# x2 turned by a DMA transpose instead of TensorE, gelu-1 remainders on VectorE, and other instruction orders, in an attention and FFN kernel

## The reference

```python
x = x + _layernorm(_L0_attn_ref(_layernorm(x), w_lhs, w_rhs))
x = x + _layernorm(_L0_ffn_ref(_layernorm(x), w1_w, w1_s, ..., w3_s))

# attention: softmax over t, no scaling
scores = jnp.einsum('nsd,ntd->nst', x * w_lhs, x * w_rhs)
return jnp.einsum('nst,ntd->nsd', jax.nn.softmax(scores, axis=2), x)

# FFN: weights are ternary (-1, 0, 1), s are scales of the outputs; hidden width 512
h = jax.nn.silu(_tlin(x, w1_w, w1_s)) * _tlin(x, w2_w, w2_s)
h = jax.nn.gelu(_tlin(h, h1_w, h1_s), approximate=False)
h = jax.nn.gelu(_tlin(h, h2_w, h2_s), approximate=False)
return _tlin(h, w3_w, w3_s)
```

## Time and profile before

| | before |
|---|---|
| time, median of 3 runs | 520.17 us (519.22 to 520.48) |
| time of the profiled execution | 520.69 us |
| its span, first to last instruction | 518.9 us |
| busy: PE / PE weight load / DVE / ACT / POOL | 469.5 / 350.3 / 366.9 / 405.8 / 314.0 us |
| share of the span | 90% / 68% / 71% / 78% / 61% |
| chain that ended last | PE 83%, ACT 6%, DVE 5%, POOL 2%, DMA 1% |
| mean granted TensorE clock | 0.975 |
| DMA | 11.83 MB, mean 23 GB/s |

### The profile page before, as it was taken

The page is one execution under the profiler, slowest core; times in us unless marked ns, Lnnn a source line. Parts: engine busy times, 40 slices in busy tenths (PEclk is TensorE's granted clock), DMA queues, the critical chain, the costliest instruction groups (busy, mean ns, idle before and its releaser), DMA issues.

```text
span 518.9 us, 8118 instructions
## 1 busy us (share of the span) xinstructions
PE 469.5 (90%) x2626; PEld 350.3 (68%) x2626; DVE 366.9 (71%) x1144; ACT 405.8 (78%) x715; POOL 314.0 (61%) x332
## 2 busy tenths in 40 slices
PE   0557599999999999999999999999999999989892
PEld 0355368686868777786868686777778686858571
DVE  3558695977777796969787777869695868654422
ACT  3343398979899898979898998989797989886871
POOL 4313409376684939395866849393958666575464
PEclk9977799999999999999999999999999999999997
DMA  8000000001010000101010100001000000000001
GB/s 302 2 1 23 21 1 1 21 1 40 3 42 0 22 21 0 42 1 42 1 42 2 40 1 22 20 2 42 1 21 0 22 3 20 1 20 2 21 1 40
DMA packets 5659, 11.83 MB, mean 23 GB/s; under 512 B 752, under 2 KB 752, under 8 KB 5616
## 3 DMA queue, kind: packets, MB, share of 16 engines
q1 hardware_dynamic: 5616, 11.28, 6.4%
HBM read 7.09 MB, written 4.19 MB: 22 GB/s over the span
## 4 chain that ended last, share of the span: by engine, by line
PE 83%; ACT 6%; DVE 5%; POOL 2%; issue 2%; DMA 1%; POOLq 0%; SPq 0%; ACTq 0%; DVEq 0%
PE hid_bank L290 46%; PE score_bank L222 8%; PE hid_bank L222 8%; PE score_bank L227 4%; PE score_bank L290 4%; PE score_bank L244 3%; PE score_bank L257 3%; PE score_bank L259 3%; PE score_bank L258 3%; DVE hA L1031 2%; ACT L803 1%; DVE row_max L992 1%; DMA columns<-columns_dram 1%; DVE max_diag L996 1%; ACT gate L764 1%
## 5 line engine op out<-in xcount | busy, mean ns | idle before, releaser
L290 PE MATMUL hid_bank<-hA_hi,w_hi 128*128 128x512 f32 x256 | 108.7, 425 | 1.4 <-DVE hA L1031 1.4
L1367 POOL TENSOR_TENSOR hB_lo<-hB,hB_hi 128x512 fp32r<-128x512 f32 x64 | 81.0, 1289 | 45.5 <-ACT hB_hi L775 45.4
L290 PE MATMUL hid_bank<-hB_hi,w_hi 128*128 128x512 f32 x256 | 101.5, 396 | 0.0
L290 PE MATMUL hid_bank<-hB_lo,w_hi 128*128 128x512 f32 x256 | 101.5, 396 | 0.0
L290 PE MATMUL hid_bank<-hA_lo,w_hi 128*128 128x512 f32 x256 | 101.2, 395 | 0.0
L1372 POOL TENSOR_TENSOR hC_lo<-hC,hC_hi 128x512 fp32r<-128x512 f32 x64 | 80.7, 1284 | 7.1 <-ACT hC_hi L775 7.1
L774 ACT ACTIVATE hC<-hid_bank,columns 128x512 f32<-128x512 f32 x64 | 44.5, 696 | 31.4 <-PE hid_bank L290 31.4
L1333 POOL TENSOR_SCALAR ln_y_var_eps<-ln_y_mean_var 128x4 f32<-128x4 f32 x16 | 3.5, 217 | 102.2 <-DVE ln_y_mean_var L959 102.2
L1031 DVE SCALAR_TENSOR_TENSOR hA<-hid_bank,columns,gate 128x512 f32<-128x512 f32 x64 | 47.6, 747 | 22.2 <-ACT gate L764 22.2
L803 ACT ACT_TABLE_LOAD x47 | 60.3, 1283 | 1.5 <-PEq L1532 0.7
L290 PEld LDWEIGHTS hid_bank<-hA_hi,w_hi 128*128 128x128 f32 x256 | 48.3, 189 | 13.1 <-DVE hA L1031 3.2
(11 more groups left out here) (85 smaller groups left out, 1150.1 us busy)
## 6 DMA issues: line engine op xcount, KB each, us to landing
x_in<-x_dram SPq DMA_DIRECT2D x16, 256.0 KB, 2.6
out_dram<-y_out SPq DMA_DIRECT2D x16, 256.0 KB, 2.0
w_raw<-weights_dram SPq DMA_DIRECT2D x5, 512.0 KB, 6.0
w_raw<-weights_dram SPq DMA_DIRECT2D x1, 256.0 KB, 5.1
columns<-columns_dram SPq DMA_DIRECT2D x1, 9.5 KB, 4.5
```

Of the source, the lines that this page charges most:

```text
L290: mm = nc.tensor.matmul(bank[:, :], lhs, rhs, start=(k == order[0] and n == 0), stop=(k == order[-1] and n == len(pairs) - 1))
L1367: nc.gpsimd.tensor_tensor(hB_lo[:, m, :], hB[:, m, :], hB_hi[:, m, :].bitcast(f32), ALU.subtract).then_inc(hB_lo_ready[m], 1)
```

## The change

Five edits.

1. **x2's transpose.** PE no longer turns x2. ACT writes the high half of `x2n` straight from SBUF into `x2_split[:, 0]` (`high_x2`, fp16), DVE the low half into `x2_split[:, 1]` (`low_x2`), and one DMA transpose from the SP queue turns both halves (128 x 1024 fp16, 256 KB) into `x2T[b % 2]`. `gated` waits for its landing.
2. **Low halves of the first gelu** (`low_B`) move from POOL to DVE, four per batch, in all batches. `low_C` stays on POOL.
3. **Orders.** The order of blocks within a sum (`SCORE_ORDER`, `BLOCKS`, `ORDER1`, `ORDER2`, `ORDER3`) may now differ by batch, and all five lists are rearranged. Batches 0 to 2 and 13 to 15 have lists of their own. The attention of a batch is spread over four places in the step instead of three.
4. **Start.** The SP queue loads weight part 2 and then x(0) first. POOL takes the first root before the weight remainders.
5. **Small ones.** `normalize_y` writes into `y_out`, and `add_ffn` adds in place. A helper `keep_warm` (matmuls that only occupy TensorE) is defined, with a POOL memset for its operand, and nothing calls it: TensorE waits in its gaps as before.

```diff
+        x2_split = sb("x2_split", [P, 2, S], f16)
+        x2T = sb("x2T", [P, TWO, 2, T, P], f16)
-        y_n = sb("y_n", [P, T, D], f32)
...
         @block.sync
+            def turn_x2(b):
+                sp.wait_ge(x2_lo_ready, b + 1)
+                after(sp, gated_mm[GATED_ORDER[b - 2][-1]], b - 1)
+                sp.dma_start_transpose(x2T[:, b % TWO, :, :, :].rearrange("p h t s -> p (h t) s"),
+                                       x2_split[:, :, :].rearrange("p h s -> p (h s)")).then_inc(
+                                           x2T_landed[b % TWO], 16)
-            def start():
-                load_weights(1)
-                load_weights(0)
-                load_columns()
-                load_weights(5)
-                load_weights(4)
-                load_x(0)
+            load_weights(2)
+            load_x(0)
+            load_weights(5)
+            load_weights(0)
+            load_columns()
+            load_x(1)
...
         @block.tensor
-            def turn_x2(b):
-                pe.wait_ge(x2n_ready, b + 1)
-                turn(x2T_bank, x2n[:, :, :], x2T_turned)
...
-                if m == GATED_ORDER[0]:
-                    pe.wait_ge(x2T_lo_ready, b + 1)
+                if m == GATED_ORDER[b][0]:
+                    pe.wait_ge(x2T_landed[b % TWO], 16 * (b // TWO) + 16)
+                hi, lo = (x2T[:, b % TWO, half, :, :].rearrange("p t s -> p (t s)") for half in range(2))
...
         @block.scalar
-            def high_x2T(b):
-                act.wait_ge(x2T_turned, b + 1)
-                after(act, gated_mm[3], b)
-                nc.scalar.copy(x2T_hi[:, :], x2T_bank[:, :]).then_inc(x2T_hi_ready, 1)
+            def high_x2(b):
+                act.wait_ge(x2n_ready, b + 1)
+                after(act, x2T_landed[(b - 1) % TWO], 16 * ((b + 1) // TWO))
+                nc.scalar.copy(x2_split[:, 0, :], flat(x2n)).then_inc(x2_hi_ready, 1)
...
         @block.vector
-            def low_x2T(b):
-                dve.wait_ge(x2T_hi_ready, b + 1)
-                minus(x2T_lo[:, :], x2T_bank[:, :], x2T_hi[:, :]).then_inc(x2T_lo_ready, 1)
+            def low_x2(b):
+                dve.wait_ge(x2_hi_ready, b + 1)
+                minus(x2_split[:, 1, :], flat(x2n), x2_split[:, 0, :]).then_inc(x2_lo_ready, 1)
+            def low_B(b, m):
+                dve.wait_ge(gelu1_done[m], b + 1)
+                nc.vector.tensor_tensor(hB_lo[:, m, :], hB[:, m, :], hB_hi[:, m, :].bitcast(f32),
+                                 ALU.subtract).then_inc(hB_lo_ready[m], 1)
...
         @block.gpsimd
             def start():
-                rest_gated()
-                low_gated()
                 rstd(ln_x, 0)
                 high_xn(0)
-                rstd(ln_x, 1)
+                rest_gated()
                 low_xn(0)
...
-                low_B(0, 0)
-                low_B(0, 1)
-                low_B(0, 3)
-                low_B(0, 2)
```

More of the change, by code:

```diff
@@ L228, in turn, with keep_warm @@
                 mm.then_inc(done, 1)
+            def keep_warm(count):
+                for n in range(count):
+                    nc.tensor.matmul(hid_bank[3][:, :], minus_ones[:, :], hC_lo[:, 0, :], start=True, stop=True)
             def turn_x(b):
@@ new lines, in start @@
+                gated(1, 1)
+                find_max(3, 0)
+                spread_max(3, 3)
+                spread_max(3, 0)
+                low_A(1, 0)
+                gated(1, 2)
+                low_A(1, 1)
+                find_max(3, 2)
+                find_max(3, 1)
+                spread_max(3, 2)
+                spread_max(3, 1)
+                gated(1, 3)
+                low_A(1, 2)
+                x1_statistics(2)
+                low_A(1, 3)
+                low_e(3, 3)
+                normalize_x(4)
@@ new lines, in start @@
+                low_xT(4)
+                low_aT(4)
+                aggregate(ln_x, 5)
+                normalize_att(3)
+                find_max(4, 3)
+                gated(2, 0)
+                gated(2, 1)
+                find_max(4, 0)
+                low_A(2, 0)
+                spread_max(4, 3)
+                spread_max(4, 0)
+                gated(2, 2)
+                low_A(2, 1)
+                find_max(4, 2)
+                find_max(4, 1)
+                spread_max(4, 2)
+                spread_max(4, 1)
@@ new lines, in start @@
+                gated(2, 3)
+                low_A(2, 2)
+                x1_statistics(3)
+                low_A(2, 3)
+                low_e(4, 3)
+                normalize_x(5)
+                aggregate(ln_x1, 3)
+                y_statistics(1)
+                low_e(4, 0)
+                low_e(4, 2)
+                low_e(4, 1)
+                low_B(2, 1)
+                normalize_x1(3)
+                low_B(2, 0)
+                aggregate(ln_y, 1)
+                low_B(2, 3)
+                low_B(2, 2)
@@ new lines, in start @@
+                normalize_y(1)
+                low_x2(3)
+                attention_statistics(4)
+                aggregate(ln_att, 4)
+                x_statistics(6)
+                low_xT(5)
+                low_aT(5)
+                aggregate(ln_x, 6)
+                normalize_att(4)
+                find_max(5, 3)
+                gated(3, 0)
+                gated(3, 1)
+                find_max(5, 0)
+                spread_max(5, 3)
+                low_A(3, 0)
+                spread_max(5, 0)
@@ new lines, in start @@
+                gated(3, 2)
+                low_A(3, 1)
+                find_max(5, 2)
+                find_max(5, 1)
+                spread_max(5, 2)
+                spread_max(5, 1)
+                gated(3, 3)
+                low_A(3, 2)
+                x1_statistics(4)
+                low_A(3, 3)
+                low_e(5, 3)
+                normalize_x(6)
+                aggregate(ln_x1, 4)
+                low_e(5, 0)
+                y_statistics(2)
+                low_e(5, 2)
```

1582 lines of the change are left out of this document (1096 added, 486 removed).

## The result

The changed kernel takes **497.4 us** (median of 4 runs, 494.6 to 499.9) against 520.3 (519.2 to 520.9): ratio 0.956, 95% interval 0.950 to 0.962. The forecast was 502, range 497 to 514. It is faster by 23 us where 18 were expected. Four single executions further down, slower than the fastest of their kernel by 1.5% or more (674.1 us with two transposes, 582.6 with three, 575.0 with low_B on POOL, 2637.2 with the gaps filled), count in none of the medians.

What follows compares the result with a forecast made beforehand. PE bounds the steady batch; at both ends order and latency of single operations count. Span 518.9 - 10.5 (start and ramp) - 4.3 (steady) - 3.1 (end) = 501.0, + 1.8 - 0.5 gives 502 us, range 497 to 514.

Steps and rivals of the forecast that it cites:

- the likeliest case: Whole kernel: the forecast itself, 502 us with its own range of 498 to 506, chance 0.67.
- Transpose, taken at 4.0 us: x2's 256 KB DMA transpose, every batch: 4.0 us, hidden under 6.4 of steady cover, costing nothing.
- The turn off PE, 0.44 us a batch: Steady batch on PE: dropping x2's four transposes and the slow matmul behind them saves 0.36 + 0.08 = 0.44 us.
- The steady part, -4.3: First gated block of batch 1 to batch 14's: turn gone, one more attend interruption, net -0.33 us over 13 batches.
- low_B on DVE, costed at nothing: Four subtractions moved to DVE: 25.2 of 28.1 us busy, tightest cover 0.3 to 0.4 us, no cost.
- The rival of DVE's order: Steady batches: DVE becomes the bound by its order, 29.2 us a batch, 516 in full, 506 to 514 in part; chance 0.14.
- The start, -6.4: Earlier x(0) load and first root: xn(0) starts at 8.2 us instead of 14.61, carried through the first attentions.
- The ramp, first gated block at 50.8, layer1 at 57.9: Before batch 1: x2(0) turned during attend(1), layer1 at 57.9 instead of 68.09, -10.2 us including the start.
- The end, -3.1: Last batches: -1.2 us for each of two batches and -0.7 at the very end, together -3.1.
- twice 1.2 us in the silu chain: Last two batches: x2T operand already there, silu table loaded earlier, PE restarts layer1 about 1.2 us earlier in each.
- The very end: POOL's four last low_C: new layer2 order finishes bank 3 two pairs sooner, all but the last out of the way, -0.7 us.
- POOL 80 us less, DVE 44 more: Busy time, a sign of being right: POOL about 80 us less busy and DVE 44 more.

Runs made afterwards that it cites:

- two transposes: Changed kernel with each batch's DMA transpose done twice, the second issued after the first landed: 512.5 us, ratio 0.986.
- three: Changed kernel with each batch's DMA transpose done three times, one after another: 573.8 us, ratio 1.107.
- low_B on POOL: Changed kernel with the four low halves of gelu 1 back on POOL, behind the root for y: 568.2 us, ratio 1.089.
- the gaps filled: Changed kernel with keep_warm matmuls occupying PE in gaps of the first 45 us: 498.2 us, ratio 0.958.
- the shifted kernel: Kernel before with the four shift matmuls one layer1 pair later on PE in the repeated step: 527.1 us, ratio 1.013.
- the first trace: Profiled execution of the changed kernel in its first measurement: 496.15 us; median there 497.4 us.
- the second trace: Profiled execution, at 500.3 us, of the changed kernel run again without edit; median there 498.75 us, ratio 0.958.

## Why the prediction was right, and where its terms were off

The forecast came out for the mechanisms that it named, but the number has some luck in it. 497.4 lies just inside the range (its lower bound was 497), two of the four executions lie below that bound, and the likeliest case had a range of its own from 498. In the profiled execution the three terms are off by -3.6, -4.7 and +1.4, so they partly offset each other. The experiments isolate the start (6.0 us) and the turn (6.4 us) of the 23. The rest is read from the traces: no run has the new orders without the DMA transpose, or the transpose without the new orders.

- **Transpose, taken at 4.0 us:** measured 3.1. It is hidden in 15 of 16 batches (in batch 0, where it takes 4.4, the cover is 5.4). The steady cover, laid out as 6.4, is 6.2. For batch 14 I laid out 2.4 us of cover and 1.9 more of a wait for ACT: the cover is 2.3, 0.94 us of waiting appear, and taking them away only brings the wait for ACT and DVE back, so they cost nothing, as I had it. "X-Bar Transpose (TRN2)" in the Trainium skill's "Advanced Engine Details and Errata" (transposes as fast as regular transfers) fits the 3.1 beside 2.8. The figure of the Trainium skill's "VectorE: DVE Perf Modes" (section "The three transpose paths") for one block can't be multiplied by eight blocks: that estimate was 10.5.
- **The turn off PE, 0.44 us a batch:** right (0.42 by putting it back).
- **The steady part, -4.3:** this is the term that was mis-sized; it is -9.0. From the earlier trace rows to the window above a steady batch gains 0.53 us, not 0.33. The step that failed is that I counted only what PE drops and adds. Split by the distances of the starts, the turn gives -0.43, one more attend interruption and a turn of x that stands apart from attend cost +0.13, and -0.22 come from the shifts, which before started 0.11 late and took 0.11 longer. I had no term for waits of 0.1 us since no row shows them as idle. That they are due to DVE's order is supported by the shifted kernel, where the wait stays; that 0.22 of it is gained here is a reading of starts, which no run isolates. Thirteen batches at 0.53 make 6.9. The other 2.1 us are the first and the last step of the stretch (27.01 instead of 29.12, 26.79 instead of 28.41), less the step before the last (28.53 instead of 28.44). Their contents were rearranged; I have not separated them.
- **low_B on DVE, costed at nothing:** right here, but for a narrower reason than I gave. The sum of busy time (25.2 forecast, 24.8 measured) says little. In the kernel before the same move costs 17 us, and in the new order to leave it undone costs 37 at the better of two places. The rival of DVE's order was real, and decided by which of DVE's results PE waits for. The cover at low_A(2), laid out as 0.4 us, is about 0.2.
- **The start, -6.4:** xn starts 6.56 us sooner in the trace; by itself the start is worth 6.0.
- **The ramp, first gated block at 50.8, layer1 at 57.9:** 46.78 and 54.89 in the first trace, 50.51 and 58.59 in the second. The difference is the clock, which I took as low for the scores ahead of the gated block. At the low clock of the second trace the stretch up to batch 1 is -10.4 for a forecast of -10.5. So the term is right for the slower case, and 3.7 us of the excess gain come and go between executions.
- **The end, -3.1:** -1.7. Of the twice 1.2 us in the silu chain the one of batch 15 lies inside this stretch and came (23.43 to 22.15 us between the two gated blocks). The one of batch 14 did not: its wait lies in the stretch ahead, and there PE still waits 0.94 us for the turned x2, where it waited 1.02. The step that failed for it is "now the operand is there". The very end gave 0.43 of 0.7.
- **POOL 80 us less, DVE 44 more:** -60 and +36. The low halves did move 81 and 44 us. The rest of POOL's work takes 20 us more, the cast of xn most of all (1052 instead of 610 ns, sixteen times); it stands beside other work of DVE now (see the last section for such a meeting; I did not isolate it here). The rest of DVE's takes 8 less, which I didn't follow up.

## What to carry to other kernels

A transfer that replaces work on the bound engine is judged by two numbers: issue to landing, and its cover, the time from the issue to the first read of its result, batch by batch. Below the cover it was free here, above it cost more than its excess (20 us for each us in 16 batches), since in some batches the clock fell behind the gap. Moving an operation to a faster engine has no price of its own: the same four subtractions cost nothing, 17 us or (left undone) 37, depending on what stands behind them in that engine's list and which result the bound engine asks for first. And waits of 0.1 us showed as no idle time; compare the distances of starts, sum them by kind of instruction, and multiply by the number of batches.

## What the runs showed of the hardware

**DVE and POOL hold each other up.** A low half takes DVE 0.69 us alone. In six steady batches of the first execution the first `hB_lo` takes 0.84 beside POOL's work; in one batch of the second the first two take 2.75 together. DVE and POOL in such a batch of the changed kernel (second execution):

```profile
291.07 2.75 DVE L1533 TENSOR_TENSOR hB_lo<-hB,hB_hi 128x512 fp32r<-128x512 f32 x2 [0.41 <-ACT hB_hi L1182]
...
288.16 1.74 POOL L2013 TENSOR_SCALAR ln_x_var_eps<-ln_x_mean_var 128x4 f32<-128x4 f32 x1 [7.90 <-DVE ln_x_mean_var L1450]
...
290.96 1.29 POOL L2052 TENSOR_TENSOR y_out<-y_out,x 128x512 f32<-128x512 f32 x1
292.19 1.08 POOL L2033 CAST xn_hi<-xn 128x512 f16<-128x512 f32 x1
```

A 128x4 operation that takes POOL 0.54 us at this place in the neighbouring batches takes 1.74 while DVE makes `e_lo`, so `y_out` begins just ahead of `hB_lo` (290.96 and 291.07). The first `hB_lo` ends 0.55 us behind POOL's `y_out`, the second 0.54 behind the cast. The batch takes 28.3 us instead of 27.9. In the kernel before with low_B on DVE a meeting of x2n with POOL's cast and `hC_lo` comes in every steady batch and costs 1.35 us (2.46 less 1.11). The Trainium skill's "SBUF — State Buffer", section "SBUF: two separate sides", says that VectorE and GpSimd share one pair of ports as an exclusive lock for a whole instruction; the traces agree in these two meetings, with the numbers above. Not every pair of operations meets so: in before x2n (227.55 to 228.66) takes 0.34 us a piece beside POOL's root (227.76 to 228.77).

**A transpose of 256 KB is almost a plain transfer** in time (3.1 us), but it occupies the SP queue for 1.24 us at its issue, against 0.33 for a load in the steady part, and the share of busy time of the DMA engines rises from 0.06 to 0.14 in a steady batch.

**The clock after a gap was not settled by the length of the gap.** Behind the same idle times the same kernel ran at 1.00 once and near 0.5 another time, and gaps of 3 us in each batch lowered it in some batches only.
